# Key sums and attention in one block, first batch's rows loaded early, key blocks of the sums a tile sooner

## Time and profile before

| | before |
|---|---|
| median of 3 runs | 1273.97 us (1273.5 to 1274.87) |
| the profiled execution | 1277.79 us |
| its span | 1276.0 us |
| PE busy | 1190.6 us, 93% |
| DVE, ACT, POOL busy | 879.2, 738.2, 536.0 us |
| one tile's values on PE, start to start | 0.71 us (L104 to L106, six matmuls) |
| one tile's features | 0.94 us (L292, eight matmuls) |
| one group of sums | 1.47 us (L309, 96 matmuls) |
| one key block or key projection | 1.36 us (six matmuls) |
| one query projection | 1.22 us (six matmuls) |
| last step of the first block | begins at 303.8 us |

### The profile page before, as it was taken

One profiled execution on the slowest core, in us unless ns is written; L12 is line 12 of the kernel. 1 busy time (PEld: TensorE's weight loads), 2 busy tenths in 40 slices (PEclk: granted clock), 3 DMA queues, 4 the chain that ended last, 5 costly groups with the idle time before them and its releaser, 6 DMA issues.

```text
span 1276.0 us, 28260 instructions
## 1 busy us (share of the span) xinstructions
PE 1190.6 (93%) x10014; PEld 1056.9 (83%) x10014; DVE 879.2 (69%) x1950; ACT 738.2 (58%) x1330; POOL 536.0 (42%) x561
## 2 busy tenths in 40 slices
PE   5999999999877999999999999999999996998888
PEld 4888888888757878888788888887888896887888
DVE  5666666666647888787878878788777644666664
ACT  4656556566555666666576665766666643544432
POOL 2423232233235354463653635535445764633400
PEclk9999999999988999999999999999999998998999
DMA  4211111110031111011001110111001024023000
GB/s 142 75 43 44 53 32 42 54 40 1 2 80 67 49 47 52 1 48 48 19 30 48 48 48 0 48 48 37 11 0 50 18 105 133 2 67 108 1 9 8
DMA packets 42689, 56.12 MB, mean 44 GB/s; under 512 B 3410, under 2 KB 41602, under 8 KB 42626
## 3 DMA queue, kind: packets, MB, share of 16 engines
q1 hardware_dynamic: 41810, 54.23, 13.5%
q10 hardware_dynamic: 816, 1.05, 0.3%
HBM read 54.81 MB, written 0.46 MB: 43 GB/s over the span
## 4 chain that ended last, share of the span: by engine, by line
PE 57%; DVE 7%; DMA 2%; issue 2%; ACT 2%; SPq 1%; POOL 1%; DVEq 0%; ACTq 0%
PE att_bank L104 16%; PE att_bank L106 14%; PE att_bank L105 14%; PE att_bank L1857 6%; PE att_bank L1815 3%; DMA att_raw_n<-in_ctx 1%; DVE att_cn L2112 1%; DVE att_pr L2166 1%; DMA tail_x<-in_x 1%; SPq L1293 1%; DVE tail_full L1431 1%; PE att_bank L1569 1%; DVE tail_hid L1450 0%; PE att_bank L942 0%; PE att_bank L1387 0%
## 5 line engine op out<-in xcount | busy, mean ns | idle before, releaser
L2338 POOL TENSOR_TENSOR att_sq<-att_work,att_sq 128x500 fp32r<-128x500 f32 x90 | 119.8, 1331 | 159.8 <-DVE att_sq L2132 159.8
L2342 POOL TENSOR_TENSOR attention_kk<-att_work,attention_kk 128x500 fp32r<-128x500 f32 x90 | 122.0, 1355 | 153.0 <-DVE attention_kk L2140 153.0
L104 PE MATMUL att_bank<-att_pT,att_cn 125*128 125x448 f32 x384 | 157.1, 409 | 7.2 <-DVE att_pT L2181 6.6
L1995 ACT ACTIVATE att_pr<-att_pr,att_nmx 112x1500 f32<-112x1500 f32 (+1 forms) x96 | 108.5, 1130 | 71.0 <-DVE att_nmx L2169 71.0
L106 PE MATMUL att_bank<-att_pT,att_cn 125*128 125x448 f32 x384 | 140.9, 367 | 0.0
L105 PE MATMUL att_bank<-att_pT,att_cn 125*128 125x448 f32 x384 | 140.4, 366 | 0.0
L2181 DVE TENSOR_TENSOR att_pT<-att_bank,att_pT 125x448 fp32r<-125x448 f32 x192 | 118.1, 616 | 14.5 <-ACT att_pT L2011 14.3
L537 DVE SCALAR_TENSOR_TENSOR attention_kk<-kvs_keys_ps,kvs_bk,attention_kk 64x500 fp32r<-64x500 f32 x96 | 70.9, 738 | 81.5 <-ACT attention_kk L421 79.9
L2166 DVE TENSOR_SCALAR_CACHE_REDUCE att_pr<-att_bank 112x500 f32<-112x500 f32 x192 | 121.7, 675 | 6.3 <-PE att_bank L106 4.9
L1857 PEld LDWEIGHTS att_bank<-all_ident,att_pr 112*125 112x125 f32 x768 | 109.6, 189 | 14.3 <-ACT att_pr L1995 2.3
L292 PE MATMUL kvs_feat<-kvs_f,attention_kk 128*125 128x256 f32 x768 | 112.6, 285 | 6.3 <-DVE attention_kk L537 6.2
(11 more groups left out here) (279 smaller groups left out, 3421.4 us busy)
## 6 DMA issues: line engine op xcount, KB each, us to landing
attention_raw_t<-in_ctxT SPq DMA_DIRECT2D x45, 500.0 KB, 3.9
att_raw_n<-in_ctx SPq DMA_DIRECT2D x16, 750.0 KB
kvs_raw_q<-in_wq SPq DMA_DIRECT2D x8, 256.0 KB, 3.9
tail_wo_raw<-in_wo SPq DMA_DIRECT2D x4, 512.0 KB, 4.4
tail_down_w<-in_down SPq DMA_DIRECT2D x8, 256.0 KB, 4.0
tail_gate_w<-in_gate SPq DMA_DIRECT2D x7, 256.0 KB, 2.9
tail_up_w<-in_up SPq DMA_DIRECT2D x7, 256.0 KB, 3.2
tail_gate_w<-in_gate SPq DMA_DIRECT2D x1, 1760.0 KB, 7.1
```

The lines of the kernel that those rows point to most:

```text
L104: nc.tensor.matmul(out, w_lo, x_hi, start=start, stop=False, skip_group_check=True)
L1995: nc.scalar.activation(pr[:, j, keys], pr[:, j, keys], ACT.Exp, scale=-1.0, bias=nmx[:, j:j + 1], accum_out=z[:, 4 * u + j, c:c + 1]).then ...
L2338: nc.gpsimd.tensor_tensor(sq[1][:, i % 2, :], work[:, i % 2, :], sq[0][:, i % 2, :].bitcast(F32), ALU.subtract).then_inc(sq_lo, 1)
L2342: nc.gpsimd.tensor_tensor(kk[:, c, 2 + gi, :], work[:, i % 2, :], kk[:, c, gi, :].bitcast(F32), ALU.subtract).then_inc(k_lo, 1)
```

## The change

Both blocks become one: the programs of `sums_and_queries` are returned as functions and run at the head of the second block's programs. The barrier, the clearing of the semaphores and the second table load between them go; POOL clears the spent semaphores after its part of batch 0. `eps`, `mean_mat` and `z` are set at the start, and `bv`, `tmp`, `sums_sb` live on. SP issues the two row loads of batch 0 after its last loads of the first part. `raw_w`, `x` and `xn` share memory with `raw_n`. The last turn runs on TensorE inside the first scores, `read_blocks` on DVE after their third group, and rows are cast in all four groups. In the first part the key blocks and the context's splits stand a tile sooner, the queries' operations stand ahead of the key blocks' evictions on ACT and DVE, and the first batch's keys start at tile 5, with the two banks exchanged, and end within tile 11.

```diff
-        FIRST_KEYS_AT, NK = 6, 2 * KC
+        FIRST_KEYS_AT, NK = 5, 2 * KC
...
-        def split_at(i, last, t):
+        def split_at(i, first, last, t):
             c, n = divmod(t, TPC)
-            if n != 1 or (last and c > 0):
+            if n != (1 if first and c == 0 else 0) or (last and c > 0):
                 return []
...
-        def keys_at(i, last, t):
+        def keys_at(i, first, last, t):
             c, n = divmod(t, TPC)
             if last:
-                return {0: [(i, 1, 0)], 2: [(i, 1, 1)], 3: [(i, 2, 0)], 5: [(i, 2, 1)]}.get(t, [])
-            if n not in (0, 2):
-                return []
-            return [(i, c + 1, n // 2)] if c + 1 < KC else [(i + 1, 0, n // 2)]
+                return {0: [(i, 1, 1)], 2: [(i, 2, 0)], 4: [(i, 2, 1)]}.get(t, [])
+            if n % 2 == 0:
+                return [(i, 1, 0)] if first and t == 0 else []
+            m = c + (1 if n == 1 else 2)
+            return [(i, m, (3 - n) // 2)] if m < KC else [(i + 1, m - KC, (3 - n) // 2)]
...
             load_heads(B - 1)
+            sp.wait_ge(w_lo, 2)
+            sp.wait_ge(turned_done, DC)
+            for half in range(2):
+                rows = slice(half * (SK // 2), (half + 1) * (SK // 2))
+                sp.dma_start(raw_n[:, half], a["ctx"][0:1, rows, :].rearrange("a (j p) c -> p (a j) c", p=KP))\
+                    .then_inc(n_loaded[half], 16)
+            sp.wait_ge(t_lo, B * KC)
...
                 if n == 0:
-                    pe.wait_ge(proj_free, NH + 1)
                     pe.wait_ge(ks_lo, 4 * B * KC)
+                if n == 1:
+                    pe.wait_ge(proj_free, NH + 1)
...
                     values(i, t)
+                    if last and t == KT - 1:
+                        key_mean(NK - 1)
                     features(i, t)
...
-                    for which in keys_at(i, last, t):
+                    for which in keys_at(i, first, last, t):
                         keys(*which)
-                    if last and t > FIRST_KEYS_AT:
-                        key_mean(t - FIRST_KEYS_AT - 1)
-                    if last and t >= FIRST_KEYS_AT:
-                        key_project(t - FIRST_KEYS_AT)
                     for k, h in queries_at(i, last, t, MEAN_AT):
                         mean_square(h, k)
+                    if last and FIRST_KEYS_AT < t < KT - 1:
+                        key_mean(t - FIRST_KEYS_AT - 1)
+                    if last and FIRST_KEYS_AT <= t < KT - 1:
+                        key_project(t - FIRST_KEYS_AT)
...
             add(B - 1, NG - 1)
-            key_mean(NK - 1)
-            turn(B - 1)
...
@@ scalar, step @@
-                    for which in keys_at(i, last, t):
-                        keys(*which)
...
                     for k, h in queries_at(i, last, t, SQUARE_AT):
                         square(h, k)
                     for k, h in queries_at(i, last, t, ROOT_AT[last]):
                         root(h, k)
+                    for which in keys_at(i, first, last, t):
+                        keys(*which)
...
@@ vector, step @@
-                    if not last and t > 0:
-                        for which in keys_at(i, last, t - 1):
-                            keys(*which, (1,))
-                    for which in keys_at(i, last, t):
-                        keys(*which, (0, 1) if last else (0,))
...
                     for k, h in queries_at(i, last, t, ROOT_AT[last]):
                         normalise(h, k)
+                    if t > 0 or not first:
+                        for which in keys_at(i, first, last, t - 1) if t > 0 else [(i, 1, 0)]:
+                            keys(*which, (1,))
+                    for which in keys_at(i, first, last, t):
+                        keys(*which, (0,))
+                    if last and t > FIRST_KEYS_AT:
+                        if t == KT - 1:
+                            key_high(NK - 2)
+                        key_normalise(t - FIRST_KEYS_AT - 1)
+                        if t != KT - 2:
+                            key_high(t - FIRST_KEYS_AT - 1)
...
@@ attention_and_after @@
-        FIRST_ROWS = ((), range(0, 3), range(3, 6), range(6, KT))
+        FIRST_ROWS = (range(0, 3), range(3, 6), range(6, 9), range(9, KT))
...
+                        if j % 2 == 0 and starts:
+                            pe.wait_ge(sums.k_lo, 2 * c + gi + 1)
...
+                            if starts:
+                                pe.wait_ge(sums.q0_lo, 2)
+                                pe.wait_ge(sums.v_set, B * KT)
...
+                    if starts and j == 1:
+                        sums.turn(pe, B - 1)
+                if starts:
+                    pe.wait_ge(sums.kv_done, 4 * B)
+                    pe.wait_ge(sums.kmean_free, NS)
...
                         for t in FIRST_ROWS[j]:
                             split_n(b, t)
+                        if j == 2:
+                            sums.read_blocks(dve, B - 1)
...
             batch(0, False)
+            pool.wait_ge(pv_done, 1)
+            pool.wait_ge(exp_done, 1)
+            pool.wait_ge(ring_free, NSC + 1)
+            for c in range(KC):
+                pool.wait_ge(t_loaded[c], 16)
+            nc.gpsimd.sem_clear(sums.spent)
```

More of the change, by code:

```diff
@@ L1 @@
+import collections
 import math
@@ L221, in run_peeled, with turn, read_blocks, sync @@
             step(B - 1, False, True)
-        @block.sync
-        def _(sp):
+        def turn(pe, i):
+            wait(pe, kv_taken, 4 * (i + 1))
+            for n in range(2):
+                last = nc.tensor.transpose(sums[:, 1, n * 128:(n + 1) * 128], sums_sb[:, n * 128:(n + 1) * 128],
+                                           ident[:])
+            last.then_inc(kv_turned, 1)
+        def read_blocks(dve, i):
+            wait(dve, kv_turned, i + 1)
+            src = sums[:, 1, :].rearrange("p (h n) -> p h n", n=32)
+            to = kv[:, one(context(i))].rearrange("p a h n -> p (a h) n")
+            for n in range(2):
+                r = slice(64 * n, 64 * (n + 1))
+                nc.vector.tensor_tensor(tmp[r], bv[r, :, n, :], src[r, :, HE:RV].to_broadcast([64, NP, HE]),
+                                        ALU.mult).then_inc(tmp_done, 1)
+                nc.vector.tensor_copy(to[r, :, HE], src[r, :, HE]).then_inc(kv_done, 1)
+            for n in range(2):
+                r = slice(64 * n, 64 * (n + 1))
+                wait(dve, tmp_done, 2 * i + n + 1)
+                nc.vector.tensor_tensor(to[r, :, 0:HE], tmp[r], src[r, :, 0:HE], ALU.add).then_inc(kv_done, 1)
+        def sync(sp):
             def load(i, c):
@@ L313, in add @@
                 last.then_inc(sums_done, 1)
[L315 to L321, removed]
             def turn_x():
@@ L714, in step @@
                         split_square(h, k)
-                    for which in split_at(i, last, t):
+                    for which in split_at(i, first, last, t):
                         split(*which)
@@ L735, in _ @@
             run_peeled(pool, step)
-            key_low(NK - 1)
-            pool.wait_ge(a_lo, 2)
-            pool.wait_ge(k_lo, NK)
+        numbers = [sem.num for sem in p.sems]
+        spent = range(numbers[0], numbers[-1] + 1)
+        assert numbers == list(spent)
+        for sem in p.sems:
+            nc.release_semaphore(sem)
+        done = Sums(n_loaded, k_lo, q0_lo, kmean_free, v_set, kv_done, turn, read_blocks, spent)
+        return (sync, tensor, scalar, vector, gpsimd), done
 H = 2
@@ L1749, in _ @@
         def _(sp):
+            first[0](sp)
             def load_t(b):
@@ L1892, in unit, with batch @@
                         wo.spread(pe, B - 1)
-            def batch(b, first, last):
-                scores(b, 0)
-                unit(b, 0, (b, 1), None if first else (b - 1, 1))
+            def batch(b, starts, last):
+                scores(b, 0, starts)
+                unit(b, 0, (b, 1), None if starts else (b - 1, 1))
                 scores(b, 1)
@@ L2208, in unit, with batch @@
                         split_n(keys[0], t)
-            def batch(b, first, last):
-                before = None if first else (b - 1, 1)
+            def batch(b, starts, last):
+                before = None if starts else (b - 1, 1)
                 scores(b, 0, before)
```

161 lines of the change are left out of this document (69 added, 92 removed).

## The result

The kernel after took 1285.79 us (median of 4 runs, 1284.83 to 1286.88), the kernel before in the same session 1273.74 us: a ratio of 1.0086, interval 1.0067 to 1.0105. It is **slower by 12 us** by the medians, where 16 us less were forecast. The profiled execution took 1284.83 us.

What follows compares the result with a forecast made beforehand. TensorE was taken as the bound, so only its standstills pay. Terms -7.2 + 1.8 + 1.3 - 4.3 - 7.8 gave -16.2 us; from the median of 1273.97 us the forecast was 1257.8 us, range 1252.5 to 1265.5.

Steps and rivals of the forecast that it cites:

- Two more memsets lie under DVE's wait at the start: At DVE's start: two added memsets are hidden under an existing wait; no time was counted for them.
- a code fetch: Sign that the prediction is wrong: an instruction fetch between TensorE's last sums.
- rival 4: Loop over contexts: features wait for ACT's whole queue at tile 11, 4.2 us per step, total 1280.0 us; chance 0.03.
- Loop, steps 1 to 6: Loop over contexts: feature and POOL waits shrink, a new 0.5 us wait for ACT appears; net -7.2 us.
- rival 1: Loop over contexts: the features' wait only moves to ACT, so the loop gives nothing, 1265.0 us; chance 0.2.
- First step: First context step: the second key block waits for DVE's eviction of the first; +1.8 us, between +0.5 and +2.5.
- Last step up to the last sums: Last step: waits at tiles 0 and 3 +1.3, longer standing before the key projection 1.4, late mask 1.4 us.
- Rival 2: Last step: two close stalls make TensorE's clock fall, costing up to 3.4 us, total 1261.2 us; chance 0.2.
- Seam: Between last sums and first scores: sums' copy wait, turn outside the scores and barrier idle go, 7.1 us together.
- The 2.29 us: "Issue" idle inside the sums; if it came a second time, the stretch to first scores would gain only -2.5 us.
- First scores to full speed: First score to third weighted sum: DVE sets the pace, first weighted sum at 15.9 us; -7.8 us, between -6 and -9.
- rule on the clock: TensorE's clock fell from 1.00 only in the stretches with 5.26 and 6.58 us of idle.

Runs made afterwards that it cites:

- eight memsets: Kernel after with eight memsets of an unread tile added to DVE's program at the start, ahead of the attention loop: 1258.24 us, 0.9874 of the kernel before.
- six padded forms: Kernel after with 2, 8, 121, 123, 124 or 126 padding memsets at DVE's start: 1259.28, 1258.24, 1261.11, 1259.41, 1262.00 and 1286.55 us.
- the waits removed: Kernel after with eight memsets plus five moves of ACT, DVE and POOL work, each against one traced wait: 1246.99 us, 0.9780 of the kernel before.

## Why the prediction was wrong

**The step that failed** is one that the text does not have. It follows the change to the third weighted sum and leaves all behind it as it was; of the instructions taken from and added to DVE's program ahead of the loop it says "Two more memsets lie under DVE's wait at the start". Their duration is indeed nothing. The number of instructions moves a loop of 262 instructions over an edge, and that costs 5.6 us per return, 28 us in all. Among the signs for wrong I named a code fetch, but only between TensorE's sums, from a stall that stood in the earlier trace rows. The 1.45 us of "issue" there in the kernel after is no fetch either: POOL's mask ends just before it, as predicted. No rival had this mechanism, rival 4 reached 1280.0 us by another one, and the range ended at 1265.5. That the instruction queue's packets could have been laid against the loop before the change was not considered.

**With the placement undone the forecast holds**: 1258.24 us measured, 1257.8 forecast, 16.2 us less than the kernel before of the same runs, and 16.2 was the sum. Its terms, from the table and the timelines:

- *Loop, steps 1 to 6:* -7.2 predicted; the period went from 40.46 to 38.83 us, so -9.8. No feature matmul waits for L537's successor. The new wait is there as predicted, for ACT:

```profile
PE kvs_feat L336 <- ACT kvs_kp L512: 2.7, 6, 0.5
```

  with the hidden part 0.6 us per step, against 0.5. What was sized too small is what the old waits cost; rival 1 (the wait only moves) falls.
- *First step:* +1.8 predicted, at most +2.5. The end of step 1 is 2.7 us later although that step is 1.6 shorter, so +4.3 (+3.7 with eight memsets). The wait of 1.9 us is as predicted; missed was what follows it, in the kernel after a granted clock of 0.66 from 30 to 35 us. Loop and first step together: -5.4 predicted, and the end of step 6 shows -5.7.
- *Last step up to the last sums:* 1.3 + 1.4 + 1.4 predicted longer, 4.1 us. The waits are there: 1.8 us at tile 0, 0.5 at tile 3, 2.9 before the first key projection, and 1.45 ahead of the last sums:

```profile
PE kvs_keys_ps L106 <- DVE attention_kk L572: 4.8, 2, 2.9
PE kvs_sums L353 <- issue: 1.5, 1, 1.5
```

```profile
324.00:328.00 4.00, 3.71 (x14) 3.19 (x15) 0.24 (x1) 0.68 (x1) 0.00 (x0) 0.58 0.00 0
```

  From the end of step 6 the last group of sums starts 2.1 us later than before in the kernel after, and 3.5 to 5.3 us later in its six padded forms. Rival 2 (the clock falls in the last step), with chance 0.2, is what happens, at the projection behind the 2.9 us: shortly in the kernel after, as the window shows, and at 0.79 for 14 us in the padded one.
- *Seam:* -7.1 predicted, -7.4 measured, scores directly behind the sums. The 2.29 us did not come a second time; the bound for that case was added up wrongly (-4.3 + 2.29 is -2.0, not -2.5), and nothing rests on it.
- *First scores to full speed:* -7.8 predicted. First weighted sum 15.3 us after the first score (15.9 predicted, 22.8 before), and the end of the loop's first iteration 167.8 us after it, where it was 176.0: -8.1.
- *Behind the loop:* the tail behind the attention loop took 314.3 us, 316.1 with eight memsets and 316.2 before; up to 2 us that no term covers.

The terms that were off, the first step (+2.5) and the loop (-2.6), cancel by luck.

The prediction's rule on the clock says that it fell only in the stretches with 5.26 and 6.58 us of idle. That holds for the rows shown; the kernel before's clock also falls eight times in the tail (slices 34 and 37 of its row), and here it fell to half at 324 us, behind 2.9 us of standing.

## What to carry to other kernels

When a change adds or removes instructions ahead of a long loop, count that loop's instructions on each engine and lay the instruction queue's packets beside the trace: idle time "issue" just behind the loop's head, and a packet count that has grown by a multiple of the iterations, mean that the loop no longer fits, and a few memsets under an early wait are both the test and the repair. Compare the time at several events of both traces before judging a change by its total: here every intended part worked. And when a table moves work to other tiles, look at what shares the new tile, since an order within it that was worth nothing may now decide.

## What the runs showed of the hardware

- DVE's blocks of instructions here have 8192 bytes, and a loop body of 262 instructions costs nothing or 5.6 us per iteration: with 124 and 126 memsets of padding 1262.0 and 1286.6 us. Counted by the trace's records the edges lie alike in both programs; counting in the compiled programs alone misled me.
- A stall of DVE of 3.4 us became 4.9 us of standing on TensorE and then 6.8 us at half clock (529 to 536 us; matmuls of 0.62 us, not 0.39), in each of five iterations. Without the stall TensorE stands 1.4 us at this place (the kernel with eight memsets):

```profile
528.99 0.48 PE L106 MATMUL att_bank<-attention_kk,attention_q 128*112 128x500 f32 x1 [1.43 <-DVE att_pr L2197]
```

  So 3.5 us of standing and, for 13 distances of 0.42 in place of 0.23 us, some 2.5 us of half clock make 6.0 us; the first iteration behind such a return is 5.9 us longer than with eight memsets (89.5 and 83.6).
- The kernel after and its padded forms have the same work from the end of step 6 to the last sums and take 55.5 to 58.7 us for it; the clock from 326 to 340 us differs too (0.95 in the kernel after, 0.79 to 0.88 in the padded forms). With the waits removed it is 1.00.
